# Output-projection part of the heads by 64-row products, even and odd heads side by side, the odd heads' rows placed by DMA

## What is computed

```python
for _ in range(NB):
    logits = _rms(x, norm_pre_w) @ compete_w.T + compete_b        # 16 slots
    vals, idx = top_k(swapaxes(logits, 1, 2), 4)
    written = einsum('bsk,bskd->bsd', softmax(vals), gather(x @ write_w.T + write_b, idx))
    ws = _rms(ws + written, norm_post_w)                          # (B, 16, D)
    q = (x @ wq.T + bq).reshape(B, L, 16, 64)                     # 16 heads of 64
    kk = (ws @ wk.T + bk).reshape(B, 16, 16, 64)
    vv = (ws @ wv.T + bv).reshape(B, 16, 16, 64)
    att = softmax(einsum('blhd,bshd->bhls', q, kk) / 8)
    ctx = einsum('bhls,bshd->blhd', att, vv).reshape(B, L, D)
    x = _rms(x + ctx @ out_proj_w.T + out_proj_b, norm_post_w)
```

## Time and profile before

| | us |
|---|---|
| median of three runs | 1033.46 |
| lowest, highest | 1032.94, 1034.28 |
| the profiled execution, its own time | 1033.91 |
| its span in the profile | 1031.8 |
| B part and the scores behind it, round 0 | 419.88 to 437.47 |
| the same, round 1 | 777.00 to 794.59 |
| PE busy, share of the span | 95% |

### The profile page before, as it was taken

How to read it: one execution, slowest core, us unless ns; L and a number is a source line. 1 busy time by engine, 2 the same in 40 slices (tenths; PEclk the granted TensorE clock), 3 DMA queues, 4 the chain that set the end, 5 groups by cost and what they waited for, 6 DMA issues and landing times. The chain is left out here.

```text
span 1031.8 us, 15570 instructions
## 1 busy us (share of the span) xinstructions
PE 983.6 (95%) x5296; PEld 572.3 (55%) x5296; DVE 728.4 (71%) x1049; ACT 581.9 (56%) x987; POOL 427.5 (41%) x189
## 2 busy tenths in 40 slices
PE   3999999999999989999999999999799999999995
PEld 1444444444444446566666666665475666666663
DVE  6999999999999973355555555565533666667666
ACT  3888888888888842245555555556322233332332
POOL 8899999999999730000000000010100233233231
PEclk9999999999999999999999999999899999999999
DMA  5577777777776348358888888984283688888886
GB/s 166 170 228 252 239 230 253 231 239 256 230 247 222 123 128 316 117 182 284 297 293 292 290 296 291 303 264 173 103 336 137 212 284 298 297 291 303 286 295 215
DMA packets 128430, 249.35 MB, mean 242 GB/s; under 512 B 9552, under 2 KB 75984, under 8 KB 128368
## 3 DMA queue, kind: packets, MB, share of 16 engines
q1 hardware_dynamic: 127600, 246.44, 70.5%
q0 software_dynamic: 768, 2.10, 0.8%
HBM read 164.35 MB, written 83.89 MB: 241 GB/s over the span
## 5 line engine op out<-in xcount | busy, mean ns | idle before, releaser
L1144 PE MATMUL bank<-work 128*128 128x256 f32 (+1 forms) x992 | 237.0, 382 | 0.6 <-PEq L1070 0.3
L1181 PE MATMUL bank<-work 128*128 128x512 f32 (+1 forms) x504 | 226.6, 592 | 1.5 <-DVE work L1273 1.5
L953 PE MATMUL bank<-work,ident 128*128 128x512 f32 x384 | 188.6, 614 | 20.3 <-DVE work L840 19.0
L1144 PEld LDWEIGHTS bank<-work 128*128 128x128 f32 x992 | 181.3, 190 | 35.4 <-issue 16.2
L1495 POOL TENSOR_TENSOR work<-work 128x1024 f32<-128x1024 f32 x30 | 70.8, 2359 | 192.0 <-DVE work L1326 192.0
L1181 PEld LDWEIGHTS bank<-work 128*128 128x128 f32 x504 | 95.7, 190 | 95.3 <-issue 92.1
L327 POOL DMA_INDIRECT work<-x_natural_scratch,gidx x16 | 14.7, 917 | 300.9 <-DVE gidx L301 297.3
L1248 DVE TENSOR_TENSOR work<-bank,sbias 128x256 f32<-128x256 f32 x64 | 27.2, 425 | 153.1 <-PE bank L1144 144.1
L953 PEld LDWEIGHTS bank<-work,ident 128*128 128x128 f32 x384 | 65.9, 191 | 105.8 <-issue 78.1
L953 PE MATMUL bank<-work 128*128 128x511 f32 x256 | 121.2, 596 | 0.0
L832 DVE SCALAR_TENSOR_TENSOR work<-work,decay 128x512 f32<-128x512 f32 x128 | 98.9, 830 | 0.0
(11 more groups left out here) (165 smaller groups left out, 1389.2 us busy)
## 6 DMA issues: line engine op xcount, KB each, us to landing
x_natural_scratch<-work SPq DMA_DIRECT2D x64, 512.0 KB, 5.0
work<-x_natural_scratch SPq DMA_DIRECT2D x64, 512.0 KB, 4.8
work<-in_kT SPq DMA_DIRECT2D x32, 512.0 KB, 3.7
work<-in_xT SPq DMA_DIRECT2D x32, 512.0 KB, 3.9
x0T_scratch<-work SPq DMA_DIRECT2D x32, 512.0 KB, 3.2
work<-x0T_scratch SPq DMA_DIRECT2D x32, 512.0 KB, 6.3
x1T_scratch<-work SPq DMA_DIRECT2D x32, 512.0 KB, 3.0
work<-x1T_scratch SPq DMA_DIRECT2D x32, 512.0 KB, 5.8
```

The source lines that it names most:

```text
L953: return nc.tensor.matmul(ps[:, at:at + n], w, v, start=start, stop=not start, skip_group_check=True)
L1144: last = nc.tensor.matmul(ps_s[p], xTb[p][:, c, :], Amat[:, i, :, c * 32:c * 32 + 32], start=(c == 0), stop=(c == NC - 1))
L1181: last = nc.tensor.matmul(ps_o[:, cols], attT[:, k * P:(k + 1) * P], Bmat[k][:, i, cols], start=(k == 0), stop=(k == 1), skip_group_check= ...
```

## The change

- `vvz` is repacked: half as large, with no zeros. For a pair of batches r (batches 2r and 2r+1) the 32 columns of a head pair are now two batches x 16 slots. The even head's values stand in the first 64 rows, the odd head's in the last 64, with the two batches in reverse order. ScalarE's zeros for `vvz` go.
- The B part has four groups (k, r) for eight. Each head pair is two products of 64 rows (e = 0 even head, e = 1 odd head) that write the same 32 partitions of two different banks: banks 1 and 2 for groups 0 and 2, banks 0 and 3 for groups 1 and 3. The count of products stays 64.
- For each group VectorE copies the even bank to `Bmat[k][:, 2r]` (with the bias for k = 0), ScalarE copies the odd bank to a staging area `Bodd[g]` (first 4096 columns of the work area, where `wr`/`wq` lay), and ScalarE copies `Bmat[k][:, 2r]` on to batch 2r+1, from SBUF to SBUF.
- The odd heads' 16-row pieces go from `Bodd` to `Bmat` by DMA: `send_rows(g, e)` is 4 transfers of 16 rows x 4 KB, 32 transfers a round. Two calls stand at the end of the head, and one in each of the tail's steps 2 to 7. In odd batches the places of a pair's even and odd head are exchanged, and `kkz` is filled in the same exchanged order.
- Group 1 now waits for the last two products' copies, groups 2 and 3 for both copies of the group two back. The scores of tile 0 go to bank 1 and wait for three even copies. Tile 0's output product waits for the first eight row transfers, tile 7's for the other 24.
- The weight pieces are sent in steps 8 to 27, two a step in the last four; at step 8 SyncE waits for all row transfers.
- The output bias goes to 32 rows. `over_tiles` writes 8 tiles out ahead of its loop, for 4.

```diff
-        vvz = cut(44160, 1024).rearrange("p (h b s) -> p h b s", h=HP, b=B)
+        vvz = cut(44160, 512).rearrange("p (h r b s) -> p h r b s", h=HP, r=2, b=2)
-        groups = [(k, b) for b in range(B) for k in range(2)]
+        groups = [(k, r) for r in range(2) for k in range(2)]
+        Bodd = [cut(1024 * g, C) for g in range(4)]
+        def send_rows(sp, t, g, e):
+            k, r = groups[g]
+            sp.wait_ge(grp_second, 4 * t + g + 1)
+            sp.wait_ge(grp_odd, 4 * t + g + 1)
+            for j in range(4):
+                rows = slice(32 * j + S * e, 32 * j + S * e + S)
+                sp.dma_start(Bmat[k][rows, 2 * r + 1 - e, :], Bodd[g][rows, :]).then_inc(brows_in[r][e], 16)
...
-                    if g == 2:
+                    if g == 1:
+                        wait_product(pe, HP - 2)
                         wait_product(pe, HP - 1)
-                    wait_group(pe, g - 3)
+                    if g > 1:
+                        pe.wait_ge(grp_even, 4 * t + g - 1)
+                        pe.wait_ge(grp_odd, 4 * t + g - 1)
                     for half in range(2):
                         cols = slice(CH * half, CH * half + CH)
                         for j in range(4):
-                            last = nc.tensor.matmul(group_bank(g)[32 * j:32 * j + 32, cols],
-                                                    vvz[:, 4 * k + j, b, :], weights["wo"][1][4 * k + j][:, cols],
+                            for e in range(2):
+                                rows = slice(64 * e, 64 * e + 64)
+                                last = nc.tensor.matmul(group_bank(g, e)[32 * j:32 * j + 32, cols],
+                                                        vvz[rows, 4 * k + j, r, :, :], weights["wo"][1][4 * k + j][rows, cols],
...
-                wait_product(pe, HP - 2)
-                wait_product(pe, HP - 1)
                 pe.wait_ge(ob_zero, 1)
+                pe.wait_ge(grp_even, 4 * t + 3)
...
-                for g in range(1, 8, 2):
-                    k, b = groups[g]
+                def odd_rows(g):
                     act.wait_ge(grp_ps, g + 1)
-                    nc.scalar.activation(Bmat[k][:, b, :], group_bank(g)[:, :], ACT.Copy).then_inc(grp_a, 1)
+                    nc.scalar.activation(Bodd[g], group_bank(g, 1)[:, :], ACT.Copy).then_inc(grp_odd, 1)
+                def second_batch(g):
+                    k, r = groups[g]
+                    act.wait_ge(grp_even, 4 * t + g + 1)
+                    nc.scalar.activation(Bmat[k][:, 2 * r + 1, :], Bmat[k][:, 2 * r, :], ACT.Copy).then_inc(grp_second, 1)
...
+                        if isinstance(m, int) and 2 <= m < 8:
+                            send_rows(sp, t, *((0, 0), (1, 0), (2, 1), (3, 1), (2, 0), (3, 0))[m - 2])
...
+                            if isinstance(m, int) and m == 0:
+                                pe.wait_ge(brows_in[0][1], 128 * t + 128)
+                            if isinstance(m, int) and m == 7:
+                                pe.wait_ge(brows_in[0][0], 128 * t + 128)
+                                for e in range(2):
+                                    pe.wait_ge(brows_in[1][e], 128 * t + 128)
```

More of the change, by code:

```diff
@@ L363, in build @@
         Bmat = [BM[:, 4096 * k:4096 * k + 4096].rearrange("p (b x) -> p b x", b=B) for k in range(2)]
-        groups = [(k, b) for b in range(B) for k in range(2)]
+        groups = [(k, r) for r in range(2) for k in range(2)]
+        Bodd = [cut(1024 * g, C) for g in range(4)]
+        brows_in = [[sem(f"B_rows_in_{r}_{e}") for e in range(2)] for r in range(2)]
+        grp_even, grp_odd, grp_second = (sem(f"B_{v}") for v in ("even", "odd", "second"))
+        def send_rows(sp, t, g, e):
[5 more added lines that the diff above has]
+                sp.dma_start(Bmat[k][rows, 2 * r + 1 - e, :], Bodd[g][rows, :]).then_inc(brows_in[r][e], 16)
         sbias = sb("sbias", [P, B, HS])
@@ L470, in sp_program @@
                     load_rows(sp, t, m, m)
+                for g in range(2):
+                    send_rows(sp, t, g, 1)
             def project(pe, ps, xT, name, done, at, to):
@@ L557, in pe_program @@
                 pe.wait_ge(sb_ok, 1)
[L558 removed]
+                for g, (k, r) in enumerate(groups):
                     if g < 2:
@@ L635, in act_program @@
                     act.wait_ge(x1T_out, 16 * NT)
-                for z in (kkz, vvz):
-                    nc.scalar.activation(z.rearrange("p h b s -> p h (b s)"), zeros, ACT.Copy, scale=0.0)\
-                        .then_inc(kz, 1)
+                nc.scalar.activation(kkz.rearrange("p h b s -> p h (b s)"), zeros, ACT.Copy, scale=0.0).then_inc(kz, 1)
                 keys(0)
@@ L704, in dve_program @@
                 dve.wait_ge(ob_in, 16)
[L705 to L706 removed]
+                for g, (k, r) in enumerate(groups):
                     dve.wait_ge(grp_ps, g + 1)
[L708 to L709 removed]
+                    if k == 0:
+                        nc.vector.tensor_tensor(Bmat[k][:, 2 * r, :], group_bank(g, 0)[:, :], obias[:], ALU.add).then_inc(grp_even, 1)
+                    else:
+                        nc.vector.tensor_copy(Bmat[k][:, 2 * r, :], group_bank(g, 0)[:, :]).then_inc(grp_even, 1)
             h.sp_write_bias, h.sp = sp_write_bias, sp_program
@@ L1107, in step @@
                             load_residual(m - 2, p)
-                        if first and 4 <= m < 28:
+                        if isinstance(m, int) and 2 <= m < 8:
+                            send_rows(sp, t, *((0, 0), (1, 0), (2, 1), (3, 1), (2, 0), (3, 0))[m - 2])
+                        if first and m == 8:
+                            for r in range(2):
+                                for e in range(2):
+                                    sp.wait_ge(brows_in[r][e], 8 * 16)
+                        if first and 8 <= m < 28:
+                            send_weights(sp, *early[m - 8])
+                        if first and 24 <= m < 28:
                             send_weights(sp, *early[m - 4])
```

49 lines of the change are left out of this document (29 added, 20 removed).

## The result

| | kernel before | changed kernel |
|---|---|---|
| median of 4 runs | 1033.82 us | 1019.95 us |
| their range | 1032.94 to 1034.28 | 1018.61 to 1021.82 |
| profiled execution: time, span | 1033.91, 1031.8 us | 1020.55, 1018.7 us |
| its mean granted clock | 0.994 | 0.993 |

The ratio of the times is 0.9867, with a 95% interval of 0.9855 to 0.9878: 13.9 us less at the medians, 13.1 us in the spans of the profiled pair. The prediction said 1020.9 us, between 1018 and 1027.

The account below looks back on a forecast made before the run. TensorE, busy 95% of the span, was taken to bound. Per round 6.86 us fewer slots, less a 0.45 us stall and 0.1 for signals, gave 6.3; 1033.46 - 12.6 = 1020.9 us, range 1018 to 1027.

Parts of the forecast that it names:

- What bounds the kernel, and what removes it: Whole kernel: TensorE, busy 95% of the span, bounds; halving the B part's slots removes 6.86 us a round.
- Eight records a slot: B part: an even and an odd record share a slot, 16 slots of 0.428 us, 6.85 us in all.
- The wait ahead of group 3: B part: group 3 stalls 0.45 us for ScalarE's copy odd 1, which follows a second copy.
- The block's end: End of the head's block: ScalarE, now with eight copies, ends at 430.85, 0.2 us ahead of TensorE.
- The eight transfers in the head: End of the head: SyncE sends eight row transfers from 424.4 to 429.2; tile 0's output product has 3.3 us spare.
- Steps 24 to 27: First tail: moved weight pieces raise the DMA share to 1.05; queue 2 us behind, cost 0, at worst 2 us.
- The transfers in the tails: Tails' steps 2 to 7: four row transfers each take SyncE 2.4 us, with room behind them; cost 0.
- The clock: Early in head 1: the half-clock stretch costs about 2.9 us; shifted, it may cost nothing or twice that.
- 1 (four at a time): B part: eight records take two slots, so it stays 13.7 us and the kernel 1033.5 us; chance 0.06.
- 2 (a longer slot): B part: eight share a slot of 0.64 us, 10.3 us in all; kernel 1026.9 to 1028 us; chance 0.05.
- 3 (row halves take turns): B part: upper and lower half alternate and break column packing; kernel slower, 1061 or 1115 us; chance 0.06.
- 4 (copies become the bound): B part: ScalarE's chain of copies holds up the block's end, 2.2 us a round; kernel 1023 to 1027; chance 0.12.

Follow-up runs that it names:

- before_half: The kernel before with four of the B part's eight groups, products and copies, left out: 1018.31 us, ratio 0.9857.
- act_order: The changed kernel with ScalarE copying odd bank 1 ahead of its second copy for group 0: 1026.37 us, ratio 0.9902 to the kernel before.
- no_rows: The changed kernel without the second tail's 24 row transfers and tile 7's wait for them: 1024.98 us, ratio 0.9879 to the kernel before.
- small_rows: The changed kernel with the second tail's 24 row transfers cut to 16 elements of a row for 1024: 1025.98 us, ratio 0.9888 to the kernel before.
- again: The changed kernel with no edit, timed again on another chip: 1028.33 us, ratio 0.9901 to the kernel before.
- again2: The changed kernel with no edit, timed once more on another chip: 1025.25 us, ratio 0.9880 to the kernel before.
- same_half: The changed kernel with both products of a head pair taking rows 0 to 63: 1033.57 us, ratio 1.0002 to the kernel before.
- early_rows: The changed kernel with the tail's 24 row transfers sent eight a step in steps 2 to 4: 1024.94 us, ratio 0.9873 to the kernel before.
- both: The changed kernel with the edits of early_rows and act_order together: 1027.82 us, ratio 0.9907 to the kernel before.

## Why the prediction held, point by point

- **What bounds the kernel, and what removes it.** TensorE's slots in the B part. Right: before_half, which halves them and adds nothing, brings 14.6 us, 13.7 of it in the B parts.
- **Eight records a slot.** Forecast 16 x 0.428 = 6.85 us, which stands. The ground was an analogy with column parts, and the three runs confirm it: same rows, 13.94 us; no odd records, 7.28; twice the records, 13.89.
- **The wait ahead of group 3.** Forecast 0.45 us behind ScalarE's odd copy 1; measured 0.37, and act_order removes it with the order of two copies. The B part was put at 7.47 and is 7.38, the saving at 6.3 a round and is 6.49.
- **The block's end.** Forecast: ScalarE ends 0.2 us ahead of TensorE. ScalarE's rows answer to the earlier trace rows; here are its groups over 415 to 431:

```profile
L670 ACT ACTIVATE work<-work 128x1024 f32<-128x1024 f32 x4 | 4.1, 1050 | 0.3 <-DVE work L744 0.3
L665 ACT ACTIVATE work<-bank 128x1024 f32<-128x1024 f32 x4 | 4.1, 1017 | 3.0 <-PE bank L587 3.0
```

  1050 ns for a copy within SBUF, where 1.02 to 1.15 was the bound and 1.04 the value. It ends at 427.88 + 1.99 = 429.87. TensorE ends by 430.52 (426.80 + 3.72), so the margin is 0.65 us. The next product starts at 430.84, 0.32 after TensorE's end, as before: the block's end moves with TensorE. The B part's start was 0.46 earlier than in the sum, which accounts for half of the 1 us between 430.85 and 429.87. The rest is the pace of the copies: in a row they start 0.90 to 0.95 us apart (423.77, 424.67, 425.62), where the sum had 1.05 to 1.1 for each.
- **The eight transfers in the head.** Forecast 424.4 to 429.2 on SyncE, and it was 423.89 to 429.36 (5.47 us for eight, 0.68 each with the wait among them). These eight (ns to issue, least, median, most; then landing in us):

```profile
L380 SPq DMA_DIRECT2D work<-work x8: 533/589/1060, 423.9 to 428.8; - x8
...
DMA to landing us min/median/max: 2.4/2.5/2.8
```

  The issue is 0.59 as taken from the earlier trace rows. The landing was put at 4.1 and took at most 2.8, so the last had landed by 432.2; the first output product is at 435.95 and didn't wait. Those of the second tail issued from 787 to 824 took up to 7.0 us (median 5.6).
- **Steps 24 to 27.** Forecast a DMA share of 1.05 and a queue that falls behind by 2 us. The window that answers to the first of the earlier trace rows, then its busiest 9 us, then the landing of the x loads (line 398) over 637 to 668:

```profile
640.00:685.00 45.00, 45.00 (x264) 30.68 (x263) 27.15 (x52) 26.22 (x64) 3.62 (x4) 1.00 0.97 318
...
658.00:667.00 9.00, 9.00 (x53) 6.08 (x52) 6.04 (x11) 5.06 (x12) 0.00 (x0) 1.00 1.03 367
```

```profile
DMA to landing us min/median/max: 5.6/8.9/9.5
```

  Over the 45 us the share is 0.97 at 318 GB/s; in its first three parts of 9 us, at and behind the last steps with two pieces (up to 657), it is 1.00, 1.01 and 1.03. The x loads landed after 6.1 us at the median there in the kernel before and after 8.9 now. So the forecast queue is there, 2.8 us for the 2 that were put. No tile is longer: from the first output product of the first tail to the next to last it is 266.47 us in both kernels. The cost put at 0 was right, and for the reason given.
- **The transfers in the tails, put at 0: the term that was mis-sized.** The prediction looked at what stands behind the transfers in SyncE's order, which is the load of x and the store, and both had room. It did not look at the residual's loads, which lie ahead of them in that order but in flight beside them. These now land after 5.7 us for 4.8 at the median, and 7.9 for 5.3 at most. VectorE waits 6.0 us and TensorE is late by 0.87 us in the second tail. no_rows and small_rows show what makes the loads late, the bytes on the DMA engines; that the late tile follows from it has the support and the exceptions told above. The price is small since VectorE has slack: of 6.0 us of waits one reached TensorE, for 0.64.
- **The clock.** Forecast that the stretch at half clock early in head 1 would move, by 2.9 us either way. It did. Before, and then the two of after:

```profile
736.93:743.76 6.83, 5.96 (x52) 3.10 (x56) 4.43 (x9) 2.87 (x6) 2.71 (x3) 0.50 0.26 77
```

```profile
711.57:714.99 3.42, 3.42 (x5) 1.35 (x4) 0.00 (x0) 2.84 (x6) 0.00 (x0) 0.50 0.94 384
...
732.05:735.47 3.42, 3.39 (x34) 1.61 (x37) 2.57 (x5) 1.41 (x3) 1.65 (x2) 0.50 0.41 115
```

  One of 6.83 us became two of 3.42, and round 1's B part comes 0.96 us earlier behind the last output product. That can't be put down to the change, since the same kernel has the one of 6.83 us again in again and again2. What it is worth shows between the end of the idle stretch and round 1's B part: 38.0 to 38.4 us in the four profiles with 3.4 us at the lower clock there (after, same_half, early_rows, both), 38.8 to 39.6 in the ten with 6.8. The other stretch, at 711.57, costs next to nothing: from the start of the last output product to that of the last product ahead of the idle stretch it is 14.70 us, for 14.64 before, as TensorE waits less for VectorE in between. The timeline after shows what TensorE did there; it answers to the earlier trace rows:

```profile
731.25 0.44 PE L499 MATMUL bank<-ident,work 128*128 128x128 f32 x2 [4.18 <-DVE work L694]
```

  The idle time of 4.18 us ahead of it is the same in both kernels. The clock fell 0.8 us after TensorE took up work again (731.25, 732.05); in the kernel before it had fallen 0.8 us ahead of that (736.93, 737.72). In the stretch at 711.57 the DMA engines were at a share of 0.94, and VectorE had nothing to do. It has no counterpart in the kernel before.
- **The rivals.** 1 (four at a time) falls: loads come eight at once. 2 (a longer slot) falls: 0.43 us, not 0.64. That was the case worked out beside the 10.6 of the Trainium skill, page TensorE: Matmul & The Clock Gate, section Measured speedup vs the span model. By that figure as the prediction used it the B part would be 10.3 us as an estimate, and these runs show 7.4 with the factor from four to eight whole; the disagreement is with that use of it, since the page packs in another shape. 3 (row halves take turns) falls altogether: the B part has become half as long. 4 (copies become the bound) holds in kind with a price of 0.37 us a round, as the main forecast had it. The warning of the Trainium skill in TensorEngine Tiling (Array Packing), section PSUM Bottleneck, agrees with the trace in direction: 0.37 us is waited for a copy in a part that had waited for none.
- **What agreed by luck.** The two signs that weren't forecast, +0.87 in the second tail with +0.42 at the first tail's last tile, and -0.96 and -0.46 that aren't the change's, cancel nearly. The last tile's gap lies between 7.67 and 8.46 over all profiles here, so its 0.42 isn't put down to the change either. Without them the change's own part is 12.98 us of B part, for 12.6 forecast. The 0.95 us between 1020.9 and 1019.95 flatter the sum a little besides: the kernel before came at 1033.82 for the 1033.46 that the sum starts from, and the saving of the medians is 13.9 for 12.6. With the gains of 9.8 and 12.8 us on the other chips, only the B part's share in it is known to a tenth.
- **What stays open.** Writing 8 tiles ahead of the loop for 4 was not tried alone; tiles take 7.11 us in the second tail in either form. Whether the wait of 0.7 us in total and the delay in the second tail can be won back in the whole time isn't settled. Why the gain was 9.8 us in again isn't either: its profile has 17 us at the lower clock ahead of the program's end, against 6.8 in those of the first pair, but no profile of the kernel before was taken on that chip.

## What to carry to other kernels

Where a product has a block of zeros in its rows, read the pace of the weight loads: if a record with few rows costs what a full one costs, the other rows can hold a second product. It had 64 rows and banks of its own here; other splits, or both halves in one bank, were not tried. Do the odd half's copies and moves on engines with slack, and place the copy that empties a bank ahead of one that only fills memory. And when transfers are added, check the loads that are in flight beside them, not only the instructions behind them in the issuing queue.

## What was not expected of the hardware

- Row halves cost nothing beside column parts: 8 records of 64x32 share a slot of 0.43 us, alternating record by record, and eight weight loads take 0.15 us where four took 0.13. The same records in the same rows need two slots.
- The row transfers are dear for their bytes. The queue's time is 0.705 x 1031.8 x 16 = 11,639 engine-us before and 0.745 x 1018.7 x 16 = 12,143 after, so 504 more for 4.33 MB: 0.116 us a KB, where the kernel's average is 0.047. On one chip, again2 less no_rows gives 118 engine-us for 1.57 MB, 0.075 a KB. The two differ by half, so it is 1.6 to 2.5 times the average, no closer. Whether the row transfers' own packets take that time, or other packets beside them take longer, these totals can't tell.
- A stretch at the 1.2 GHz level of 3.4 or 6.8 us is there in one execution and not in another of the same kernel, early in either head. The B part of round 0 starts 1 to 3 us later with one in head 0, which is more than the effects of the small edits here. Differences under some 3 us were told apart by the trace, never by the median.
